# The routing gate of a mixture-of-experts layer, moved for five of eight token groups into the attention ahead of it

## The reference

```python
x = x + xattn0(layernorm(x), ctx_1024, mask)        # 16 heads of 16
x = x + moe(layernorm(x))
x = x + xattn1(layernorm(x), ctx_1024)
x = x + binary_ffn(layernorm(x))

def moe(x):                                          # E = 32, TOP_K = 4
    scores = softmax(x @ Wg)
    weights, indices = top_k(scores, 4)
    for e in range(32):                              # first C = 2048 pairs of e
        y[tok] += swiglu(x[tok], W1[e], W3[e], W2[e]) * w
    z = swiglu(x, Ws1, Ws2, Ws3)                     # shared expert, all tokens
    return y + z
```

## Time and profile before

| | us |
|---|---|
| three executions | 1352.62, 1360.88, 1360.91 |
| profiled execution | 1356.17 |
| its span, first to last instruction | 1354.4 |
| first attention | about 64 to 243 |
| route | about 244 to the first expert product at 473.5 |
| experts, combine, second attention, last network | 473.5 to 1354.4 |

### The profile page before, as it was taken

One profiled execution on the slowest core, in us unless ns is written; L12 is line 12 of the kernel. 1 busy time (PEld: TensorE's weight loads), 2 busy tenths in 40 slices (PEclk: granted clock), 3 DMA queues, 4 the chain that ended last, 5 costly groups with the idle time before them and its releaser, 6 DMA issues. The chain is left out here.

```text
span 1354.4 us, 26011 instructions
## 1 busy us (share of the span) xinstructions
PE 1172.3 (87%) x8528; PEld 810.8 (60%) x8528; DVE 765.4 (57%) x2032; ACT 512.3 (38%) x1049; POOL 409.5 (30%) x495
## 2 busy tenths in 40 slices
PE   7699999677682399999999448899989999999998
PEld 4378888445441277778877323788865555555554
DVE  4177778565562156666656495788873434244331
ACT  6555555222230034443433136566642222222221
POOL 5260000466575445555555344600000000000000
PEclk9899999787786799999999768899999999999999
DMA  9199100263162554445444291000000000000000
GB/s 176 24 308 392 49 2 2 82 102 95 66 216 101 190 163 148 148 147 180 152 136 118 90 371 51 14 2 2 1 2 1 16 16 17 0 15 15 16 16 16
DMA packets 100754, 123.94 MB, mean 92 GB/s; under 512 B 33984, under 2 KB 76051, under 8 KB 100631
## 3 DMA queue, kind: packets, MB, share of 16 engines
q1 hardware_dynamic: 86807, 87.98, 22.1%
q0 software_dynamic: 13824, 34.38, 7.1%
HBM read 61.78 MB, written 64.72 MB: 93 GB/s over the span
## 5 line engine op out<-in xcount | busy, mean ns | idle before, releaser
L1847 PE MATMUL psA<-H,B 128*128 128x512 f16 x1024 | 223.5, 379 | 0.0
L1774 DVE SCALAR_TENSOR_TENSOR H<-psA,H 128x512 f16<-128x512 f32 x128 | 88.3, 690 | 208.3 <-ACT H L1815 208.3
L1533 POOL DMA_INDIRECT y_rows<-YB,pair x160 | 155.5, 972 | 149.0 <-DVE YB L1588 80.9
L1815 ACT ACTIVATE H<-psA 128x512 f16<-128x512 f32 x128 | 76.4, 597 | 252.7 <-PE psA L1847 252.7
L1847 PEld LDWEIGHTS psA<-H,B 128*128 128x128 f16 x1024 | 100.2, 98 | 119.3
L1643 PE MATMUL psH<-W,XT 128*128 x640 | 168.1, 386 | 0.5 <-ACT XT L1545 0.4
L203 POOL TENSOR_SCALAR var<-mv 128x4 f32<-128x4 f32 x32 | 13.7, 429 | 508.2 <-DVE mv L197 507.1
L1206 POOL DMA_INDIRECT x_rows<-XN,slot_s x128 | 130.6, 1021 | 71.5 <-issue 43.9
L806 DVE TENSOR_TENSOR PLT<-psT,PHT 128x512 f16<-128x512 f32 (+1 forms) x192 | 113.9, 595 | 38.8 <-ACT PHT L857 38.3
L857 ACT ACTIVATE PHT<-psT 128x512 f16<-128x512 f32 (+1 forms) x192 | 94.4, 525 | 102.4 <-PE psT L916 102.4
L1643 PEld LDWEIGHTS psH<-W,XT 128*128 128x128 f32 x640 | 110.1, 192 | 12.0 <-issue 3.1
(11 more groups left out here) (249 smaller groups left out, 2039.0 us busy)
## 6 DMA issues: line engine op xcount, KB each, us to landing
XG<-x_rows SPq DMA_DIRECT2D x160, 134.0 KB
y_rows<-zero_row SPq DMA_DIRECT2D x4, 4096.0 KB, 27.5
G<-y_rows SPq DMA_DIRECT2D x7, 2048.0 KB, 10.3
x_rows<-zero_row SPq DMA_DIRECT2D x33, 134.0 KB, 8.7
X<-in_x SPq DMA_DIRECT2D x8, 512.0 KB, 7.2
QT<-in_w SPq DMA_DIRECT2D x1, 4096.0 KB
out_x<-OUT SPq DMA_DIRECT2D x8, 512.0 KB
y_rows<-YB,pair POOLq DMA_INDIRECT x160
```

The costliest lines, as they stand in the source:

```text
L1533: pool.indirect_dma_start(y_rows[:, :], bass.IndirectOffsetOnAxis(ap=pair[u // HALF][:, u % HALF:u % HALF + 1], axis=0), YB[u][:], None, b ...
L1774: dve.scalar_tensor_tensor(out=H[layer][1][:, o], in0=psA[k % 4][:], scalar=0.0, in1=H[layer][0][:, o], op0=ALU.max, op1=ALU.subtract).the ...
L1847: last = pe.matmul(psA[k % 4][:], W[:, c, o * P:(o + 1) * P], src[part][:, c], start=n == 0, stop=n == 2 * n_in - 1)
```

## The change

`RouteTail` and the per-macro gate in `route` go; a class `Gate` takes their place, with methods for one step each. Inside the first `attend` the steps of macro m are issued at step t = 4m + k of the loop: turning in two halves at k = 8 and 9, logits at 10, `shift` at 11, `pick` at 12, `index` at 13, `mark` at 15, `ranks` at 16, `place` at 17, `slots` at 18. Turning is done so for seven macros, the gate for five, and the scatter for four. The turning shares the two `psT` banks with the probabilities, in an order written down in `TURNS`; logits and ranks use free columns of the bank `psO`. Rows are made by ACT from `X` straight into one of four row buffers. The counts are kept as running positions (`base`) with the limit `edge`.

In `route` three macros are left to gate, beside the first three macros of the shared expert; `up` now rotates over three banks through the whole block (`bank`), the plan is made after the third macro, and `W2` is loaded in 16 pieces as `QT` comes free.

```diff
-ROWBUFS = 2
+ROWBUFS = 4
+GATED_EARLY, SCATTERED_EARLY, TURNED_EARLY = 5, 4, 7
+TURN_AT, LOGITS_AT, PICK_AT, RANKS_AT = 8, 10, 12, 16
@@ attend, gpsimd
                 for t in range(TILES):
                     pool.tensor_tensor(X[:, t:t + 1, :], X[:, t:t + 1, :], bo[:].unsqueeze(1),
                                        ALU.add).then_inc(biased, 1)
-                for t in range(-4, 3):
-                    tail.gpsimd(pool, t)
...
+                if gate:
+                    gate.edges(pool)
+                    for m in range(MT):
+                        gate.power(pool, m)
+                    for m in range(SCATTERED_EARLY):
+                        gate.scatter(pool, m)
+                        gate.power(pool, m + MT)
@@ attend, vector
+                def gate_reads(t):
+                    for m in gate.due(t, LOGITS_AT + 1, GATED_EARLY):
+                        gate.shift(dve, m)
+                    for m in gate.due(t, RANKS_AT + 1, GATED_EARLY):
+                        gate.place(dve, m)
+
+                def gate_steps(t):
+                    if ok(t - 3):
+                        dve.wait_ge(added, t - 2)
+                        gate.stats(dve, t - 3)
+                    for m in gate.due(t, PICK_AT, GATED_EARLY):
+                        gate.pick(dve, m)
...
+                if gate:
+                    gate.begin(dve)
-                steady(body, lambda t: tail.vector(dve, t - TILES))
+                steady(body, lambda t: tail and tail.vector(dve, t - TILES))
@@ Gate
+        def edges(self, pool):
+            pool.tensor_scalar(self.name[:], expert_id[:], 1.0, None, ALU.add)
+            pool.tensor_scalar(self.base[:], expert_id[:], float(REGION), None, ALU.mult).then_inc(self.based, 1)
+            pool.wait_ge(self.based, 1)
+            pool.tensor_scalar(self.edge[:], self.base[:], float(CAP), None, ALU.add).then_inc(self.edges_s, 1)
...
+        def begin(self, dve):
+            self.own = Steps(dve, self.own_s)
+            dve.wait_ge(self.edges_s, 1)
@@ route, tensor
+                for b in range(MACROS):
+                    if b == 1:
+                        kv.values(pe)
+                    if b < PLAN_AT:
+                        if b:
+                            pe.wait_ge(gate.l_shift, GATED[b])
+                        gate.logits(pe, GATED[b])
+                    if b == PLAN_AT:
+                        pe.wait_ge(plan_s, 1)
+                        pe.matmul(psR[:], ones[:], spread.rearrange("p k u j -> p (k u j)"), start=True,
+                                  stop=True).then_inc(plan_spread, 1)
+                    up(b, 0)
+                    if b:
+                        shared_out(b - 1)
...
+                    up(b, 1)
+                    if b + TURNED_EARLY < MACROS:
+                        rest_in(b + TURNED_EARLY)
+                    if b < PLAN_AT:
+                        if b:
+                            pe.wait_ge(gate.ranks_read, GATED[b])
+                        gate.ranks(pe, GATED[b])
+                    if b == 0:
+                        kv.keys(pe)
```

More of the change, by code:

```diff
@@ L836, in body @@
                         low(t, u, 2)
+                    if gate:
+                        gate_steps(t)
                 for h in range(2):
@@ L856, in high @@
                         act.wait_ge(pv_done, t - 1)
-                    act.activation(PHT[u][:, lo:hi], piece(u, g), ACT.Copy).then_inc(hi_out, 1)
+                    act.activation(PHT[u][:, lo:hi], piece(t, g), ACT.Copy).then_inc(hi_out, 1)
                 def context_out(t):
@@ L974, in attend @@
         st.close()
[L977 to L996, removed]
-            for t in range(MT):
-                last = dve.max(self.top[:, t, :], sc[:, t, :])
-            own.done(last)
-            for t in range(MT):
-                last = dve.max_index(self.idx[:, t, :], self.top[:, t, :], sc[:, t, :])
-            own.done(last)
-            own.done(dve.tensor_copy(self.idf, self.idx[:, :, 0:TOPK]))
-            own.done(dve.tensor_tensor(
-                self.hot, self.idf.unsqueeze(3).to_broadcast([P, MT, TOPK, EXPERTS]),
-                expert_id[:].unsqueeze(1).unsqueeze(1).to_broadcast([P, MT, TOPK, EXPERTS]), ALU.is_equal))
-        def mark(self, dve, picked):
-            with nc.allow_low_precision("zeros and ones"):
-                dve.tensor_reduce(self.chosen, self.hot.rearrange("p t k e -> p t e k"), X_AXIS,
-                                  ALU.add).then_inc(picked, 1)
@@ new lines, in route, with bank @@
+        h_done, silu_s, hs_s, z_done, z_added, w2_in, plan_s, plan_spread, plan_read, w3_in = (
+            sem(s) for s in ("h_done", "silu", "hs", "z_done", "z_added", "w2_in", "plan_ready", "plan_spread", "plan_read", "w3_in"))
+        tails_s, tails_st = sem("tails_ready"), sem("tails_stored")
+        own_s, plan_own = sem("own"), sem("plan_own")
+        GATED = list(range(GATED_EARLY, MACROS))
+        PLAN_AT = len(GATED)
+        def bank(m, o, j):
+            return (4 * m + 2 * o + j) % 3
@@ L1211, in _ @@
-                for m in range(MACROS):
-                    body(m, m % ROWBUFS)
+                kv.blanks(pool)
+                for m in range(SCATTERED_EARLY, MACROS):
+                    if m + MT < MACROS:
+                        gate.power(pool, m + MT)
+                    gate.scatter(pool, m)
                 for b in range(ROWBUFS):
-                    pool.wait_ge(scattered[b], SCATTERS * len(range(b, MACROS, ROWBUFS)))
+                    pool.wait_ge(gate.scattered[b], SCATTERS * len(range(b, MACROS, ROWBUFS)))
@@ new lines, in silu, with rest_out @@
+                    act.activation(SG[:, o], psH[bank(m, o, 0)][:], ACT.Silu).then_inc(silu_s, 1)
+                def rest_out(m):
+                    act.wait_ge(gate.turned, 2 * m + 2)
+                    act.activation(QT[:, :, m * MW:(m + 1) * MW], psX[:], ACT.Copy).then_inc(gate.xt_out, 2)
+                for m in range(TURNED_EARLY, MACROS):
+                    for h in range(2):
+                        gate.apply(act, m, h)
+                for b in range(MACROS):
+                    if b < PLAN_AT:
+                        gate.exps(act, GATED[b])
+                    silu(b, 0)
+                    if b < PLAN_AT:
+                        gate.tops(act, GATED[b])
+                    if b == 0:
```

631 lines of the change are left out of this document (335 added, 296 removed).

## The result

The changed kernel takes 1421.5 us (median of four runs, 1410.6 to 1426.7); the kernel before has 1358.95 in its four. The ratio is 1.0458, with a 95% interval of 1.0379 to 1.0537: **slower by 4.6%**, where I forecast 1341 us, faster by 1.3%. The profiled execution took 1425.9 us with a span of 1424.0.

What follows compares the result with a forecast made beforehand. Attention was taken as PE-bound, route as bound by POOL, row buffers and the gate's chain. Experts starting 22 us earlier, less 4 for late signals, gave 18 us less than before: 1341 us, range 1316 to 1372.

Steps and rivals of the forecast that it cites:

- the attention's end: First attention: tile work ends near 309, POOL's scatters are 8 us late, route starts at 318.5 in place of 244.
- The term for late results: Route: PE signals reaching DVE 12.8 and 24.0 us late, unexplained, might recur; taken as 4 us, ends 0 and 37.
- What bounds the kernel: Before the change: attention bound by PE with POOL idle; route by POOL, two row buffers and the gate's chain.
- The new wait: Attention's start: DVE's maxima of tile 1 wait for POOL's `gate_edges`, +21.4 us, then +4 for PE's low clock.
- The gate's steps: In the attention: gate work on DVE and PE adds 41 us, or 7.0 us a step from step 15 on.
- Route: Route stage: bound by PE, with a 10 us wait for the plan; 133 us in place of 229.5.
- Rival 3: Route: both late signals recur on the path, 22 us gained become 37 lost, 1376 us; chance 0.14.
- The rest of the sum: Whole kernel: experts start at 451.5, 22 us earlier; with 4 us for late signals, 18 us less, 1341 us.
- The base: Old route's 229.5 us, experts from 473.5, taken as the reference for the 22 us gain.

Runs made afterwards that it cites:

- the kernel with all pauses: Changed kernel with `edges` ahead of the bias additions and a pause after every second scatter, in attention and route; 0.9607 of the kernel before, 0.9605 on another chip.
- the burst with rows written: Kernel before plus 24 back-to-back scatters of zeros, rows written, in the first attention; 1371.5 us against 1346.7.

## Why the prediction was wrong

The step that failed is the attention's end: it let four rounds of scatters run beside PE at no cost to PE. The runs show 17 to 19.5 us lost for each round. The term for late results, put at 4 us, was the same error met in route: it came to some 60 us in the attention and 31 in route.

- **What bounds the kernel**: right as far as it went. It missed that the issue of scatters itself slows PE, although both results of the earlier trace rows lay in unbroken rows of scatters: the second, at 406.7, in the one from 377.4 to 430.7, and DVE went on at 433.0, 2.3 us behind the last of them. (A small slip: two of the slices 7 to 13 of the earlier trace rows read 8, not 7 or 6.)
- **The new wait**: right. Forecast 21.4 us and maxima at 91.6, with 4 for the clock; found, in the changed kernel's timeline:

```profile
91.09 1.50 DVE L837 TENSOR_REDUCE mx<-psS 128x8 fp32r<-128x616 f32 x2 [22.16 <-POOL edge L1126]
```

  Taking it away gave 26 us (with 13 to either side), against 25.4.
- **The gate's steps**: sized too high. A step takes 6.0 us from 151.35 and 6.6 from 175.37, not 7.0, and PE is still the busier engine there (25.4 of 26.3 us, DVE 23.7). In the kernel with all pauses the last projection starts 37 us later than before (277.8 against 240.4), where the sum had 39.6 for the steps; but some 9 of these 37 are lost in the paused rounds, where four steps take 28.4 to 29.6 us. On the chip with 1304 us they take 25.8 beside the same paused rounds. So the gate's own steps cost nearer 28 us, and the agreement with 39.6 is luck.
- **The attention's end: here the sum failed.** I wrote that "the tile work itself would end near 309, so POOL is late by 8 us", with a round of 20.8 us that PE doesn't feel. The round takes 20.4 us, and PE loses 17 to 19.5 of them. Slots of macro 3 come at 331.3 in place of 292.4, and the last projection starts only at 360.9, where I had the tile work ended near 309 and route begun at 318.5. I priced what DVE does to a scatter (0 to 3 us a round; the longest took 1.79 us, beside eight DVE products with both inputs in SBUF, most 0.97) and not what scatters do to PE.
- **Route**: 133 us forecast, from the barrier on. With all pauses it takes 141 from the last projection (277.8) to the experts (418.7), and PE's one wait for the plan is 10.1 us where I had 10. Without them it takes 173, with a wait of 34.4 us. The plan itself is slowed, in a chain of small steps on DVE that wait for no other engine. The changed kernel's DVE, then the same steps with pauses:

```profile
454.09 0.23 DVE L1416 TENSOR_TENSOR lew<-le,B 128x64 f32<-128x64 f32 x1 [1.17 <-DVE le L1414]
455.49 0.22 DVE L1417 TENSOR_REDUCE ej<-le 128x2 f32<-128x64 f32 x1 [1.17 <-DVE lew L1416]
...
458.29 0.16 DVE L1419 TENSOR_TENSOR sj<-tile_id,sj 128x2 f32<-128x2 f32 x1 [2.45 <-remote]
459.69 0.17 DVE L1420 TENSOR_SCALAR aj<-sj 128x2 f32<-128x2 f32 x1 [1.24 <-DVE sj L1419]
```

```profile
352.32 0.22 DVE L1422 TENSOR_TENSOR lew<-le,B 128x64 f32<-128x64 f32 x1
352.58 0.22 DVE L1423 TENSOR_REDUCE ej<-le 128x2 f32<-128x64 f32 x1
...
352.96 0.16 DVE L1425 TENSOR_TENSOR sj<-tile_id,sj 128x2 f32<-128x2 f32 x1
353.15 0.17 DVE L1426 TENSOR_SCALAR aj<-sj 128x2 f32<-128x2 f32 x1
```

- **The term that I couldn't explain**: taken as 4 us with ends 0 and 37, in route alone. It wasn't a lateness that comes by chance but, on all chips but one, the price of each unbroken round, and the change moved 64 scatters from a stage where PE idles to one where PE is the bound. Rival 3 named the right thing with the wrong place and size (1376); its argument against, that PE kept busy would suffer less, is the reverse of what the runs show.
- **The rest of the sum**: without the wait and the late results my sum is 1341 - 25.4 - 4 = 1312, 0.965 of 1358.95; the kernel with `edges` first and a pause after every second scatter has 0.9607 and 0.9605, and starts the experts at 418.7 where the sum without the wait gives 426.1. Part of the agreement is the luck named above: gate steps sized some 10 us too high stand for what is still lost in the paused rounds.
- **The base**: I took the 229.5 us of the old route as its work. It held late results too. On the chip without them the old kernel starts the experts at 444.1, and the changed one with pauses, `edges` behind the additions as in my sum, at 439.0. Of the 22 us that I forecast, 5 are left when both are free of late results (the changed one has pauses in its route, the old one none).

## What to carry to other kernels

On every chip here but one, a stream of indirect DMAs on POOL without breaks was not free for the other engines. Put a small instruction and a wait after every second one, which cost 4 us over 128 scatters where POOL had most to do, and only then move it under work that is bound by PE. Compare on more than one chip. An unexplained late result in a trace is a term of its own: look at what every other engine was doing in that stretch before moving that work anywhere. And a wait placed behind 22 us of another engine's work costs what it says; the order of three tiny instructions was worth 26 us.

The version with both, `edges` first and the pauses, beats the kernel before by 3.9% on two chips (and by 4.2% in one run on a third). On the chip without late results it was not run; its relative with pauses in the attention only has 2.0% there, in one run.

## What the runs showed of the hardware

- Scatters of 128 rows that start every 1.28 us (0.97 us each, 0.30 between) cut PE to 1.5 to 1.9 products per us, in two stages with different products, with and without rows written. With a pause after each (1.9 us apart) no "remote" wait is left; two in a row and a pause lose little; three in a row do harm. In the experts' stage of the kernel before, scatters start 1.27 to 3.65 us apart and PE is busy 97%.
- One chip of those used shows none of this in route, with 64 scatters in one row and PE issuing 290 products in 84 us. Its experts' stage takes 264 to 265 us in three kernels, elsewhere it takes 270 to 290; whether the scatters of that stage are the cause no run shows.
- It isn't PE alone: DVE, some 25 us into route's last row of scatters, got one or two instructions every 1.4 us or more. The granted clock is lower in the bursts too (0.53 and 0.57), where PE is busy under half of the time.
- The Trainium skill (SBUF — State Buffer, "Who interferes with whom") says that PE and ACT never wait on anyone. For their ports to SBUF no run here speaks against it. Taken as a rule on what may run beside PE it fails on all chips here but one: in the burst with rows written PE issued 43 products in 23 us.
- Open: the mechanism. That an engine runs on for some microseconds and then gets a few instructions per scatter looks as if POOL's preparing kept the engines from being fed, or their signals from being passed on; the runs don't tell these apart. Every execution here has a span and a clock on record, so a part of the recording in the effect can't be excluded. What sets the one chip apart is open too, and since it was used at one time only, so is whether it is the chip or the hour.
